# Softmax denominators summed on VectorE and GpSimd instead of TensorE, in a causal attention and FFN kernel

## What is computed

```python
paths = sigmoid(x @ Wp + bp).reshape(B, T, H, 5).transpose(0, 2, 1, 3)
agree = pq * pk + (1.0 - pq) * (1.0 - pk)        # of query and key paths
sim = cumprod(agree, axis=-1).sum(axis=-1) / 5
attn = softmax(where(mask, -inf, sim), axis=-1)  # causal
ctx = einsum('bhqk,bhkd->bhqd', attn, V)
x = layernorm(x + ctx @ Wo)
h = silu(x @ wg.T) * (x @ wu.T)
x = layernorm(x + h @ wd.T)
```

## Time and profile before

| | before |
|---|---|
| median of 3 runs | 953.42 us (953.01 to 960.25) |
| profiled execution, time | 955.83 us |
| its span, first to last instruction | 954.1 us |
| mean granted TensorE clock | 0.969 |
| busy: TensorE / VectorE / ScalarE / GpSimd | 848.8 / 478.6 / 455.7 / 227.4 us |

### The profile page before, as it was taken

One profiled execution on the slowest core, in us unless ns is written; L12 is line 12 of the kernel. 1 busy time (PEld: TensorE's weight loads), 2 busy tenths in 40 slices (PEclk: granted clock), 3 DMA queues, 4 the chain that ended last, 5 costly groups with the idle time before them and its releaser, 6 DMA issues.

```text
span 954.1 us, 15450 instructions
## 1 busy us (share of the span) xinstructions
PE 848.8 (89%) x6146; PEld 412.9 (43%) x6146; DVE 478.6 (50%) x1020; ACT 455.7 (48%) x721; POOL 227.4 (24%) x265
## 2 busy tenths in 40 slices
PE   4389998899989999899988999899988998999764
PEld 3144354443644446344544436344453434444332
DVE  2844346535455426645465355555275353545343
ACT  2255644555445554546445453555546453555211
POOL 0011131223212132122312232132321223231312
PEclk9599999999999999999999999999999999999968
DMA  6831443140511433113431406104321214100000
GB/s 211 213 97 45 89 89 111 45 90 23 141 59 45 111 66 107 72 43 70 89 111 45 89 23 152 70 23 111 82 74 45 64 48 109 47 1 23 1 22 24
DMA packets 44346, 71.09 MB, mean 75 GB/s; under 512 B 3568, under 2 KB 21232, under 8 KB 44272
## 3 DMA queue, kind: packets, MB, share of 16 engines
q1 hardware_dynamic: 44272, 70.07, 28.0%
HBM read 53.28 MB, written 16.78 MB: 73 GB/s over the span
## 4 chain that ended last, share of the span: by engine, by line
PE 73%; ACT 9%; DVE 9%; issue 4%; POOL 3%; DMA 2%; SPq 0%; POOLq 0%; ACTq 0%; DVEq 0%
PE ctx_ps L717 14%; PE misc L752 13%; PE den_ps L717 12%; PE slot L695 11%; PE misc L762 9%; PE misc L671 7%; PE misc L729 6%; ACT probs L409 6%; POOL work L364 2%; PE misc L680 2%; DVE work L548 2%; DVE x L531 1%; ACT work L421 1%; DVE ctx_raw L480 1%; DMA query_stack<-phi_dram 1%
## 5 line engine op out<-in xcount | busy, mean ns | idle before, releaser
L409 ACT ACTIVATE probs<-slot 128x1024 f32<-128x1024 f32 (+3 forms) x384 | 290.3, 808 | 376.4 <-PE slot L695 376.2
L695 PE MATMUL slot<-query_stack,key_stack 128*128 128x512 f16 (+3 forms) x768 | 161.7, 333 | 16.5 <-DMA query_stack<-phi_dram 15.1
L717 PE MATMUL ctx_ps<-probs,vz_sb 128*32 128x512 f32 (+3 forms) x1536 | 166.3, 505 | 10.3 <-DVE ctx_raw L480 8.3
L364 POOL TENSOR_TENSOR work<-work 128x512 f16<-128x512 f32 x96 | 112.7, 1174 | 216.0 <-ACT work L427 215.9
L717 PE MATMUL den_ps<-probs,ones 128*32 128x512 f32 (+3 forms) x1536 | 162.8, 495 | 0.0
L355 POOL TENSOR_SCALAR_AFFINE_SELECT probs<-probs 128x512 f32<-128x512 f32 x128 | 81.8, 641 | 303.9 <-ACT probs L409 302.9
L548 DVE SCALAR_TENSOR_TENSOR work<-work,misc 128x512 f32<-128x512 f32 x96 | 65.8, 686 | 172.7 <-ACT work L421 172.7
L752 PE MATMUL misc<-x1T_hi,w_parts 128*128 128x512 f16 x384 | 147.0, 383 | 5.2 <-DVE x1T_lo L538 2.4
L752 PE MATMUL misc<-x1T_lo,w_parts 128*128 128x512 f16 x384 | 146.5, 382 | 0.0
L695 PEld LDWEIGHTS slot<-query_stack,key_stack 128*128 128x128 f16 x768 | 56.8, 98 | 170.4 <-issue 120.9
L762 PE MATMUL misc<-w_parts,work 128*128 128x256 bf16 x768 | 89.1, 273 | 10.6 <-POOL work L364 10.6
(11 more groups left out here) (52 smaller groups left out, 609.8 us busy)
## 6 DMA issues: line engine op xcount, KB each, us to landing
key_stack<-phi_dram SPq DMA_DIRECT2D x64, 256.0 KB, 5.8
query_stack<-phi_dram SPq DMA_DIRECT2D x64, 256.0 KB, 6.5
xT_sb<-in_xT_dram SPq DMA_DIRECT2D x8, 1024.0 KB, 5.1
x_sb<-in_x_dram SPq DMA_DIRECT2D x8, 1024.0 KB, 5.5
out_dram<-x SPq DMA_DIRECT2D x16, 512.0 KB, 2.9
phi_dram<-phi_hi SPq DMA_DIRECT2D x16, 256.0 KB, 2.0
phi_dram<-phi_lo SPq DMA_DIRECT2D x16, 256.0 KB, 2.3
work<-in_wgT_dram SPq DMA_DIRECT2D x1, 768.0 KB, 8.2
```

What stands on the lines that cost most here:

```text
L364: pool.tensor_tensor(hid_lo[:, n % M1, :], hid[:, n % HSLOTS, :], hid_hi[:, n % M1, :], ALU.subtract).then_inc(hid_lo_ready, 1)
L409: act.activation(probs[:, s % P_SLOTS, 2 * p:2 * p + 2, off:CH], slot[p][:, :, off:CH], ACT.Exp).then_inc(slot_drained[p], 1)
L695: mm = pe.matmul(slot[p][:, k, off:CH], key_stack[:, h, P * j:P * (j + 1)], query_stack[:, h, CH * c + off:CH * (c + 1)], start=True, stop ...
L717: mm = pe.matmul(sums[32 * k:32 * k + 32, off:CH], w, probs[:, s % P_SLOTS, k, off:CH], start=first, stop=final)
```

## The change

- `weigh` keeps the context's matmuls only. ctx_ps has two banks, one for even and one for odd chunks, and ctx_raw is gone.
- A new tensor acc [128, 4, 512] in SBUF takes the sum of a chunk's probabilities over its steps. VectorE adds step s - 1 at the start of slot s (`sum`); the chunk's first two steps are added in one instruction, with a copy of the first columns in short chunks. In long chunks steps j = 2 and j = 4 are added by GpSimd (`pool_sum`), in their own slot, in GpSimd's queue behind that slot's mask. All additions of a chunk go one after the other by the semaphore `summed`.
- After the last weigh of a chunk TensorE multiplies acc with ones once (`den`, four matmuls of 512 columns) into a `misc` bank, which it takes in turn like the others. normalise reads the denominators there and the context straight from ctx_ps.
- exps waits, besides for weigh, for the sum of three steps before. The first sum of a chunk waits until the last chunk's den is done.

In the diff, add_up with `pool.` is GpSimd's, the part with `dve.` VectorE's, and `denominator` TensorE's.

```diff
+    POOL_SUMS = [i for i, (q, c, g, j) in enumerate(STEPS) if c == 1 and j in (2, 4)]
...
+        if 1 <= s <= B * NS:
+            plan += [("sum", *divmod(s - 1, NS))]
+        if b < B and i in POOL_SUMS:
+            plan += [("pool_sum", b, i)]
         plan += between(b, i)
...
+                    plan += [("den", b, q), ("normalise", b, q)]
...
+            def add_up(b, i):
+                s = NS * b + i
+                if i in DIAG:
+                    pool.wait_ge(masked, len(DIAG) * b + DIAG.index(i) + 1)
+                else:
+                    for p in range(2):
+                        pool.wait_ge(slot_drained[p], s + 1)
+                pool.wait_ge(summed, SUMMED[b, i] - 1)
+                pool.tensor_tensor(acc[:, :, :], acc[:, :, :], probs[:, s % P_SLOTS, :, :],
+                                   ALU.add).then_inc(summed, 1)
...
+                    act.wait_ge(summed, SUMMED[b2, i2 + (STEPS[i2][3] == 0)])
...
+                if j == 1:
+                    if NQ * b + q >= 1:
+                        k, n = MISC[("den", *divmod(NQ * b + q - 1, NQ))]
+                        dve.wait_ge(misc_filled[k], n + 1)
+                    first = probs[:, (s - 1) % P_SLOTS, :, :]
+                    if off:
+                        dve.tensor_copy(acc[:, :, 0:off], first[:, :, 0:off]).then_inc(summed, 1)
+                    dve.tensor_tensor(acc[:, :, off:CH], first[:, :, off:CH], own, ALU.add).then_inc(summed, 1)
+                else:
+                    dve.wait_ge(summed, SUMMED[b, i] - 1)
+                    dve.tensor_tensor(acc[:, :, off:CH], acc[:, :, off:CH], own, ALU.add).then_inc(summed, 1)
...
-                for sums, taken in ((ctx_ps, ctx_out), (den_ps, den_out)):
...
+                if first and NQ * b + q >= 2:
+                    pe.wait_ge(ctxT_ready, NQ * b + q - 1)
...
+            def denominator(b, q):
+                pe.wait_ge(summed, SUMMED[b, LAST[q]])
+                n = claim("den", b, q)
+                for k in range(4):
+                    mm = pe.matmul(misc[n][32 * k:32 * k + 32, :], ones[:, :], acc[:, k, :], start=True, stop=True)
+                mm.then_inc(misc_filled[n], 1)
```

More of the change, by code:

```diff
@@ L137, in attention @@
             b, i = divmod(s - LAG, NS)
-            plan += [("weigh", b, i)] + [("normalise", b, q) for q in range(NQ) if LAST[q] == i]
+            plan += [("weigh", b, i)]
+            for q in range(NQ):
+                if LAST[q] == i:
+                    plan += [("den", b, q), ("normalise", b, q)]
         return plan
@@ L149, in seq_postln_kernel @@
     for what, *n in PLAN:
-        if what in ("scale", "vz", "turn_f", "project", "turn_x1", "gate", "up", "down"):
+        if what in ("scale", "vz", "turn_f", "project", "turn_x1", "gate", "up", "down", "den"):
             k = len(MISC) % 2
@@ L153, in seq_postln_kernel @@
             misc_uses[k] += 1
+    SUMMED, pieces = {}, 0
+    for b in range(B):
+        for i in range(NS):
+            q, c, g, j = STEPS[i]
+            pieces += (0, 2 if c == 0 else 1)[j >= 1] if j <= 1 else 1
+            SUMMED[b, i] = pieces
     NORM = {tuple(n): at for at, n in enumerate([n for what, *n in PLAN if what == "stats"])}
@@ L175, in seq_postln_kernel @@
         ctxT = sb("ctxT", [P, NG, CH], F32)
-        ctx_raw = sb("ctx_raw", [P, CH], F32)
+        acc = sb("acc", [P, 4, CH], F32)
         den_turned = sb("den_turned", [P, CH // 32, 32], F32)
@@ L220, in seq_postln_kernel @@
         slot = [ctx.enter_context(nc.psum_tensor(f"slot{n}", [P, 2, CH], F32)) for n in range(2)]
[L221 to L222 removed]
+        ctx_ps = [ctx.enter_context(nc.psum_tensor(f"ctx_ps{n}", [P, CH], F32)) for n in range(2)]
         misc = [ctx.enter_context(nc.psum_tensor(f"misc{n}", [P, CH], F32)) for n in range(2)]
@@ L369, in _ @@
                     mask(*n)
+                elif what == "pool_sum":
+                    add_up(*n)
                 elif what == "rsqrt":
@@ L476, in normalise @@
                 Q = NQ * b + q
[L477 to L482, removed]
+                k, n = MISC["den", b, q]
+                dve.wait_ge(misc_filled[k], n + 1)
+                dve.transpose(den_turned[:, :, :].rearrange("p a n -> p (a n)"), misc[k][:, :])\
+                    .then_inc(misc_drained[k], 1)
+                dve.wait_ge(misc_drained[k], n + 1)
                 dve.reciprocal(den_recip[:, :, :], den_turned[:, :, 0:1]).then_inc(den_recip_ready, 1)
@@ L487, in normalise @@
                 dve.wait_ge(den_inv_ready, Q + 1)
-                dve.wait_ge(ctx_out, Q + 1)
-                dve.tensor_tensor(ctxT[:, g, :], ctx_raw[:, :], den_inv[:, :], ALU.mult)\
+                dve.wait_ge(pv_done, NS * b + LAST[q] + 1)
+                dve.tensor_tensor(ctxT[:, g, :], ctx_ps[q % 2][:, :], den_inv[:, :], ALU.mult)\
                     .then_inc(ctxT_ready, 1)
@@ L633, in _ @@
                     split_weights()
+                elif what == "sum":
+                    add_up(*n)
                 elif what == "normalise":
@@ L779, in walk @@
                         weigh(*n)
+                    elif what == "den":
+                        denominator(*n)
                     elif what == "project":
```

28 lines of the change are left out of this document (19 added, 9 removed).

## The result

| | before | after |
|---|---|---|
| median | 954.24 us (4 runs) | 1037.73 us (4 runs, 1036.8 to 1040.07) |
| ratio | | 1.0865, 95% interval 1.0815 to 1.0915 |
| span of the profiled execution | 954.1 us | 1035.8 us |
| mean granted TensorE clock | 0.969 | 0.914 |

The account below looks back on a forecast made before the run. Bound: TensorE, with VectorE or GpSimd arriving as late in three places of each batch. Profiled run 955.8, plus 29.4 (A, B, D, E seven times) and 40 (C eight times), less 2.4 to the median: 1022 us; range 940 to 1045.

Parts of the forecast that it names:

- Relief: TensorE's denominator matmuls: 15.5 us a batch go, 3.4 come back; net 12.1 a batch, 97 us in eight.
- a period of about 118 us: Sign that would show the forecast: like rows of successive batches about 118 us apart.
- C: Slot 18 to the `down` of slot 24 (25.98 us): +3.4 from the queues, +1.6 clock fall, eight times.
- B: First `down` to slot 18 (12.02 us): three denominators less, one `den` more that waits for gate's bank; +0.4.
- D: `down` of slot 24 to turn_f of slot 6 (30.81 us): VectorE busy nearly throughout; +2.2.
- E: turn_f of slot 6 to slot 10 (mean 18.0 us): -1.3 from denominators, +0.8 clock fall; -0.5.
- A: Slot 10 to the first `down` (24.07 us): 26.2 by GpSimd's queue, +2.1; a clock fall left to the range (11 us).
- 0 to 5, I take 0: First batch's slots without FFN: sums on two engines in turn against 2.8 us of TensorE a step; cost taken as 0.
- costed at nothing: Edits priced at zero, among them exps waiting for the sum of three steps before; if late, scores and TensorE would wait.
- the relief goes through: Rival: GpSimd's sum and the STTs behind it are done before TensorE arrives; 856, likely about 900 us; chance 0.1.
- The queues without the exclusion: Rival: VectorE and GpSimd mostly pass each other; 940 us, 960 with all clock falls; chance 0.2.
- the clock stays up: Rival: exclusion, but no clock fall where rows show it may stay up; 995 to 1010, within the forecast's 0.7.

Follow-up runs that it names:

- the fillers: Kernel before plus GpSimd work in slot 12 that nobody needs: a multiply of 2048 elements, 962.93 us (1.0096), or two memsets, 971.25 us (1.0175).

## Why the prediction was right

**What bounds.** At the three places where VectorE or GpSimd came as late as TensorE, or one slot before, the new waits stand: 5.24 us in slot 24, 3.73 in slot 6, and 4.67 in slot 14 instead of slot 15. The page's 73% for TensorE was no guide.

**Relief.** The 97 us of matmuls are gone, as counted; alone that is worth 69 us, with TensorE busy for 761.3 us. The sign "busy time down by some 100 us" did not show in the change itself, where it fell by 44, since more of what is left runs at half clock. The sign "a period of about 118 us" was 119.5; the prediction's own stretches add up to 119 to 120.

**Unit prices.** VectorE's 2.28 us was met, GpSimd's 4.53 lay in the range, 0.13 over the 4.4 taken.

**C.** The walk gave 3.95 for normalise, 10.65 for GpSimd's first sum, 20.15 for its second, 24.7 for VectorE's sum of step 21 and 29.4 for the last hid_lo. The trace has, from 354.76: 3.3, 10.2, 19.7, 24.2 and 28.5. Early by 0.4 to 0.9 throughout, 0.65 of it from normalise on; VectorE's short instructions begin some 0.08 us before the recorded end of the last one (apply at 330.22, the STT before it until 330.30), which the walk left out. The order in which the two engines' instructions go came out as walked.

**B, D, E.** +0.67, +2.7 and -0.6 against +0.4, +2.2 and -0.5. In D 1.5 us of clock fall are contained, which the sum had at C, so D's own term was too large by about 1.

**A, the step that was wrong in kind.** +3.3 against +2.1. The walk has no apply in it, so it let apply run beside GpSimd's sum at no price. It read only the masks beside apply (0.64 us in most places), which can lose little behind instructions of 0.4 us, and not apply, which can lose the whole of a long sum. In the trace of before it took 1.77 us in all beside a mask, against 1.38 alone, and that row was there to be read:

```profile
149.88 1.77 DVE L531 TENSOR_SCALAR x<-x,mv,rstd 128x256 f32<-128x256 f32 x4 [1.13 <-POOL rstd L360]
...
150.22 0.64 POOL L355 TENSOR_SCALAR_AFFINE_SELECT probs<-probs 128x512 f32<-128x512 f32 x1 [0.38 <-ACT probs L409]
```

The forecast reached 2.1 of the 3.3 us by way of hid_lo, but it is the wait for apply that stands there. The clock fall in A, which I left out, is there.

**The first batch, mis-sized.** "0 to 5, I take 0". The multiply of normalise, third chunk of the first batch, starts 10.2 us later than before; the first fence is of the kernel before, the second of the changed one:

```profile
107.07 0.69 DVE L489 TENSOR_TENSOR ctxT<-ctx_raw,den_inv 128x512 f32<-128x512 f32 x1
```

```profile
117.30 0.69 DVE L543 TENSOR_TENSOR ctxT<-ctx_ps,den_inv 128x512 f32<-128x512 f32 x1
...
58.66 0.66 ACT L438 ACTIVATE probs<-slot 128x256 f32<-128x256 f32 x2 [7.92 <-DVE acc L524]
59.19 1.87 PE L751 MATMUL slot<-query_stack,key_stack 128*128 128x512 f16 x4 [4.76 <-ACT probs L438]
...
103.52 1.97 PE L800 MATMUL misc<-ident,x 128*128 128x128 f32 x8 [6.48 <-DVE x L585]
```

Two waits of TensorE stand there, and the second is again apply behind GpSimd's sum. The first is an edit that was "costed at nothing": exps waits for a sum that comes late, since VectorE's queue still has the preparation of the weights ahead of it, and scores stands behind exps, as the prediction said it would if a sum came late. With both engines' sums tiny 2.9 us of this wait stay, so more than half of it is the order of the queue.

**Why the total came close.** From slot 10 of the second batch to slot 10 of the seventh the period grew by 8.85 us in the mean, against 9.2 in the sum, so the steady part was right, with errors that cancel: A was 1.2 us a batch too small, C 0.8 and D 1.0 too large. Between the two profiled executions lie 81.7 us, 12.3 more than the 69.4 of the sum: 10.2 in the first batch and 2 elsewhere. The medians, 83.5 apart, add another 1.8.

**The rivals.** That the relief goes through needed both sums to cost nothing: 886. "The queues without the exclusion" has no run of its own, since no kernel can be had without it; the fillers show the exclusion itself. Its size in the change is only estimated, by the 4.4 us of C that come with both engines' sums; its opposite, that the two mostly pass each other, is out. Of "the clock stays up" (995 to 1010) nothing came: it fell behind all three waits.

## What to carry over

Before work is taken from the busiest engine, look for whom it already waits a little: there the engine that is to take the work has no slack, whatever its share of busy time. Work given to VectorE and GpSimd at once isn't given to two engines where the forms listed below meet; price it as one queue, and count what is held up that the change doesn't touch. Count the first batch too, where the queues hold other work. A sum can be made to pay if it is rare and stands behind what others wait for: four pair sums a batch gave 1% when late, with a fourth buffer, and cost 4.6% when early.

## What the runs showed of the hardware

Some GpSimd and VectorE instructions kept each other out for whole instructions. On VectorE this held for additions of two SBUF tensors (3.13 us instead of 2.29) and for tensor_scalar from SBUF to SBUF (1.38 us for four, 6.73 beside an addition, 5.28 beside memsets). On GpSimd masks (0.64 to 2.49 us), subtracts (1.16 to 3.2) and the power of four elements (1.0 to 3.03) were held by VectorE's additions. Memsets were seen to hold apply; no row shows them beside an addition. VectorE's instructions with one input from PSUM were not held (the STTs took 0.67 to 0.75 us throughout). Nor was all of VectorE's work in SBUF: bn work, which reads one SBUF tensor, kept its 1.40 us beside two hid_lo, and they kept theirs, as these rows of the changed kernel show; the transposes den_inv, also from SBUF to SBUF, kept their 0.71 us.

```profile
324.67 1.40 DVE L574 BATCH_NORM_STATS2 bn<-x 128x6 f32<-128x256 f32 x4
...
324.25 2.27 POOL L388 TENSOR_TENSOR work<-work 128x512 f16<-128x512 f32 x2
```

The Trainium skill (GPSIMD Engine Reference, section 8) names two SBUF inputs or a 2-port mode of VectorE as the case for contention; the second agrees if apply ran in such a mode, which no row here tells.

Whoever began first went first. In the changed kernel's trace 155 instructions of the two engines took over 0.15 us more than the shortest of their form, and 154 of them began while one of the other engine ran. So the hid_lo at 376.18 went ahead of VectorE's sum at 376.23, and VectorE's sum of step 22, at 380.24, ahead of the mask at 380.52. The exception, an instruction of apply, began 0.02 us before GpSimd's sum and was held all the same.
